# Reordering the copies of an attention stage on one DMA queue, with the copies of the maxima issued by SP

## The reference

```python
cond = silu(c) @ wc.T + bc
sh1, sc1, g1, sh2, sc2, g2 = split(cond, 6)
h = ln(x) * (1 + sc1) + sh1
x = x + g1 * gqa_attn(h, wq, wk, wv, wo)      # softmax(q k / sqrt(32)) v, then wo
h = ln(x) * (1 + sc2) + sh2
x = x + g2 * (gelu(h @ w1.T + b1) @ w2.T + b2)
```

## Time and profile before

| | us |
|---|---|
| median of 3 runs | 1560.06 (1552.71 to 1562.45) |
| profiled execution, own time | 1565.58 |
| its span | 1563.8 |
| PE busy | 1481.9 (95%) |
| DVE / ACT / POOL busy | 800.6 / 625.1 / 576.0 |
| queue of SP: share of 16 DMA engines | 21.7% |
| queue of ACT: share | 0.2% |

### The profile page before, as it was taken

One profiled execution on the slowest core, in us unless ns is written; L12 is line 12 of the kernel. 1 busy time (PEld: TensorE's weight loads), 2 busy tenths in 40 slices (PEclk: granted clock), 3 DMA queues, 4 the chain that ended last, 5 costly groups with the idle time before them and its releaser, 6 DMA issues. The chain is left out here.

```text
span 1563.8 us, 19142 instructions
## 1 busy us (share of the span) xinstructions
PE 1481.9 (95%) x7013; PEld 1045.6 (67%) x7013; DVE 800.6 (51%) x1356; ACT 625.1 (40%) x1116; POOL 576.0 (37%) x222
## 2 busy tenths in 40 slices
PE   7889999998999999998979999999999999999996
PEld 4545556555656555654448888888788888878885
DVE  5377667776776677676544342332524242242421
ACT  5346656665575666666532322112111121211210
POOL 0027567675776677576710020110202021020202
PEclk9869999999999999999999999999999999999998
DMA  7132314233151313323053311010202001020100
GB/s 259 55 75 59 97 52 117 65 85 101 33 154 36 112 54 98 93 71 87 2 158 112 101 55 34 27 60 0 87 0 69 18 27 60 0 87 0 61 1 27
DMA packets 68309, 105.16 MB, mean 67 GB/s; under 512 B 10464, under 2 KB 19696, under 8 KB 68232
## 3 DMA queue, kind: packets, MB, share of 16 engines
q1 hardware_dynamic: 66192, 103.74, 21.7%
q10 hardware_dynamic: 2048, 0.53, 0.2%
HBM read 55.44 MB, written 16.81 MB: 46 GB/s over the span
## 5 line engine op out<-in xcount | busy, mean ns | idle before, releaser
L899 DVE TENSOR_REDUCE neg_max<-row_bank 128x1 f32<-128x512 f32 x512 | 338.5, 683 | 184.1 <-PE row_bank L1095 181.9
L768 ACT ACTIVATE probs<-key_bank 128x512 f32<-128x512 f32 x512 | 301.5, 597 | 224.5 <-PE key_bank L1108 219.6
L1463 PE MATMUL acc<-w_t,hidden 128*128 128x512 f32 x1536 | 370.6, 390 | 7.7 <-DVE hidden L1380 7.7
L1453 PE MATMUL up<-h,w_t 128*128 128x512 f32 x1536 | 370.9, 391 | 0.0
L1463 PEld LDWEIGHTS acc<-w_t,hidden 128*128 128x128 f32 x1536 | 287.3, 188 | 69.8 <-DVE hidden L1380 10.7
L1453 PEld LDWEIGHTS up<-h,w_t 128*128 128x128 f32 x1536 | 287.5, 188 | 58.7
L651 POOL TENSOR_TENSOR probs_sum<-probs_sum,probs 128x2048 f32<-128x2048 f32 x62 | 284.5, 4589 | 29.2 <-ACT probs L768 22.5
L1324 ACT ACTIVATE gelu_full<-up,bias_cols 128x512 f32<-128x512 f32 x128 | 88.3, 690 | 515.2 <-PE up L1453 515.2
L1378 DVE CAST hidden<-gelu_full 128x512 fp32r<-128x512 f32 x128 | 67.2, 525 | 443.4 <-ACT gelu_full L1324 441.7
L1108 PE MATMUL key_bank<-q_stack,k_stack 98*128 98x512 f32 x512 | 227.0, 446 | 21.4 <-DMA q_stack<-max_row 13.3
L1095 PE MATMUL row_bank<-k_stack,q_stack 96*128 96x512 f32 x512 | 212.0, 426 | 10.8 <-DVE neg_max L899 9.5
(11 more groups left out here) (117 smaller groups left out, 1069.0 us busy)
## 6 DMA issues: line engine op xcount, KB each, us to landing
q_stack<-spare SPq DMA_DIRECT2D x384, 64.0 KB, 2.0
xa<-in_x_dram SPq DMA_DIRECT2D x8, 1024.0 KB, 5.1
resid<-in_x_dram SPq DMA_DIRECT2D x8, 1024.0 KB, 7.9
x_scratch<-resid SPq DMA_DIRECT2D x8, 1024.0 KB, 4.4
xa<-x_scratch SPq DMA_DIRECT2D x8, 1024.0 KB, 5.7
spare<-in_L_cond_w_dram SPq DMA_DIRECT2D x32, 256.0 KB, 3.0
resid<-x_scratch SPq DMA_DIRECT2D x8, 1024.0 KB, 6.8
out_dram<-y SPq DMA_DIRECT2D x8, 1024.0 KB, 4.2
```

The source lines that it names most:

```text
L768: nc.scalar.activation(probs[kt][:, r, :], key_bank[r % 2][:, :], ACT.Exp).then_inc(exp_done, 1)
L899: nc.vector.tensor_reduce(out=neg_max[:, g % 2, i:i + 1], in_=row_bank[(g + i) % 2][:, :], op=ALU.max, axis=AX.X, negate=True).then_inc(ro ...
L1453: last = nc.tensor.matmul(up[j % 2][:, :], w1_t[i][:, kt, j * P:j * P + P], h[k][:, kt, :], start=(kt == 0 and n == 0), stop=(kt == KD - 1 ...
L1463: last = nc.tensor.matmul(acc[tt][:, :], hidden[j % 2][i][:, tt * P:tt * P + P], w2_t[k][:, j, :], start=(j == 0 and n == 0), stop=(j == N ...
```

## The change

On SP the copies of the maxima are added (`stack_max` moves there from ACT), and the order of the others is changed. stack_k(3) and stack_q(2) are issued in group 0, stack_q(3) in group 1, stack_q(0) in group 2, stack_q(1) in group 3. The gate and residual of sequence b - 1 are loaded in group 1 of sequence b, behind stack_q(3), after a wait for the last store; the store of b - 1 comes at the end of group 3, behind the maxima of the next sequence. ACT issues nothing any more.

```diff
                 def load_resid(b):
+                    if b > 0:
+                        sp.wait_ge(x1_stored, b * 16)
                     sp.dma_start(gate_now[:, :], gate_dram[bass.ds(b, 1), 0, :].partition_broadcast(P)
                                  .rearrange("p a d -> p (a d)")).then_inc(gate_loaded, 16)
                     sp.dma_start(resid[:, :, :], seq_dram(x, b)).then_inc(resid_loaded, 16)
...
+                def stack_max(b, g):
+                    sp.wait_ge(row_taken, row_no(b, g, ROWS) + 1)
+                    for part in range(2):
+                        row = as_f32(q_stack[STACK + part:STACK + part + 1, g, :, :])
+                        sp.dma_start(row.rearrange("o r n -> o (r n)"), as_f32(max_row[part][:, :])).then_inc(max_stacked, 16)
...
                     stack_q(u, 1)
+                    stack_max(0, 0)
                     stack_k(2)
-                    stack_k(3)
-                    stack_q(u, 2)
...
                     if has_last:
                         sp.wait_ge(keys_scored, exps_no(b, 0, 0))
-                        stack_k(HKV - 1)
+                    stack_k(3)
+                    stack_q(seq_units(b - 1, b > 1, True) if has_last else before_units(), 2)
+                    stack_max(b, 1)
+                    sp.wait_ge(keys_scored, exps_no(b, 1, 0))
                     stack_q(u, 3)
+                    if has_last:
+                        load_resid(b - 1)
                     if has_next:
                         sp.wait_ge(proj_ready, u.ready("T3"))
...
                         sp.wait_ge(proj_taken["dve"], u.taken("K"))
                         stack_k(0)
-                        stack_q(u, 0)
+                    stack_max(b, 2)
+                    if has_next:
                         sp.wait_ge(keys_scored, exps_no(b, 2, 0))
                         stack_k(1)
-                        stack_q(u, 1)
-                    if has_last:
-                        store_x1(b - 1)
-                        sp.wait_ge(x1_stored, b * 16)
-                    load_resid(b)
+                        stack_q(u, 0)
+                    stack_max(b, 3)
                     if has_next:
                         sp.wait_ge(keys_scored, exps_no(b, 3, 0))
                         stack_k(2)
-                        stack_q(u, 2)
+                        stack_q(u, 1)
+                        stack_max(b + 1, 0)
+                    if has_last:
+                        store_x1(b - 1)
...
+                    load_resid(b)
                     for j in range(RING):
                         load_weights(sp, j)
...
-                def stack_max(b, g):
-                    act.wait_ge(row_taken, row_no(b, g, ROWS) + 1)
-                    for part in range(2):
-                        row = as_f32(q_stack[STACK + part:STACK + part + 1, g, :, :])
-                        act.dma_start(row.rearrange("o r n -> o (r n)"), as_f32(max_row[part][:, :])).then_inc(max_stacked, 16)
...
-                    stack_max(0, 0)
...
-                    if n % GROUP == TURN_BEAT + 1 and after_turn:
-                        stack_max(*after_turn)
```

More of the change, by code:

```diff
@@ L587, in before, with sequence @@
                     stack_q(u, 1)
+                    stack_max(0, 0)
                     stack_k(2)
-                    stack_k(3)
-                    stack_q(u, 2)
-                def sequence(b, has_last, has_next, odd=None, is_second_last=False):
+                def sequence(b, has_last, has_next, is_second_last=False):
                     u = seq_units(b, has_last, has_next)
```

## The result

The changed kernel takes 1574.54 us (median of 4 runs, 1573.04 to 1575.9) where the kernel before took 1557.70 in the runs beside it: a ratio of 1.0083, with a 95% interval of 1.0047 to 1.0119. A second comparison of the two, further down, gave 1.0082 (1.0055 to 1.0109). The forecast was 1578, slower.

The account below looks back on a forecast made before the run. PE (TensorE) was taken to bound the kernel. Terms +22.8 + 15.4 - 13.3 - 8.8 - 1.0 = +15.1 us gave 1580.7 from the profiled 1565.6, 1575.2 from the median; 1578 was taken between, range 1556 to 1593.

Parts of the forecast that it names:

- The gate is late, DVE waits, PE waits: Group 1, sequences 1 to 7: gate lands late, delaying DVE's row maximum; PE waits 3.1 us six times, 4.2 once: +22.8 us.
- The clock: Behind PE's seven new waits in group 1: slower clock each time, 2.2 us each, +15.4 us, bounds 0 and 20.
- Store and residual away from the maxima: First scores of new sequences: all five PE waits for maxima go, 13.3 us, plus 8.8 us of slower clock: 22.1 us gained.
- ACT's issues: SP issues the maxima, so ACT loses two issues a group, 1.17 us together; gain taken as 1.0 us, bounds 0 and 5.8.
- Nothing for residual, x load and the one queue: Group 1: later residual and x load cost nothing; maxima behind them on SP's queue still land in time.
- the rival of late maxima: Group 1: maxima behind 2.25 MB on one queue land late, seven times 3.2 + 2.2 us, 1616 us; chance 5%.
- The rivals of a shorter wait: Group 1: clock stays up or gate lands early, about 1560 us, 25%; gate covered, no new wait, 1537 us, 7%.
- The sum: Whole kernel: all gains and costs together, +15.1 us on the profiled execution, 1565.6 to 1580.7; from the median 1575.2.

Follow-up runs that it names:

- the move that undoes it: Changed kernel with the gate issued ahead of the 12 copies of Q3 in group 1, the residual still behind them: 1537.34 us, ratio 0.9833 to the kernel before.
- the kernels with the gate behind nine copies and alone: Changed kernel with gate behind 9 of 12 Q3 copies: 1543.72 us; with gate behind all 12, SP awaiting its landing before residual and x load: 1561.50 us.
- The kernel with this part alone: Kernel before, ACT still issuing maxima, with group 3's store, gate and residual loads moved behind stack_k(2) and stack_q(2): 1542.46 us, ratio 0.9877.

## Why the prediction was right, and where it was off

**The gate is late, DVE waits, PE waits.** Shown in all its steps, by the timelines above and by the move that undoes it (1574.5 to 1537.3 us). In sequence 3 DVE's wait was 4.65 us (4.5 forecast) and PE's 3.24 (3.1 forecast). That they are so near is in part luck, since two errors offset each other: the 12 issues took 8.0 us instead of 7.5, and the gate landed in 4.6 us instead of 5.1. Over seven PE's waits were 24.5 us against 22.8. The q issues, of which one or two were held up in four of the seven sequences, took 3.1 us more than forecast, the landings (4.5 to 5.2 us, 4.8 in the mean, against 5.1) 2.2 us less; the other 0.8 is not traced.

**The clock.** Seven falls, as forecast, at 1.9 us each in place of 2.2: 13.5 us against 15.4. The experiments add the other side: waits of 0.76 us and of 1.4 to 1.7 us brought none in the kernels with the gate behind nine copies and alone.

**Store and residual away from the maxima.** Right in mechanism and size. The kernel with this part alone is 1542.5 us, and its profiled execution is 23 us shorter in span than that of before (1540.4 for 1563.8, of which 1.4 us are an earlier first score), where 22.1 was forecast.

**ACT's issues.** This term of the sum was mis-sized: 1.0 us taken, 5.4 measured in the first groups of sequences 1 to 7. The bound of 5.8 was too low as well. Sequence 0 and the third group of sequence 7 are each 0.5 us shorter in the changed kernel, and in the profile with ACT issuing again they were 0.3 and 0.5 us longer than in the changed one; that makes 6.3 us or so. The prediction read the wait list of PE for exponentials and judged that few of its entries stood behind an issue. What it should have read is ACT's own timeline in the beats of the issues. In group 0 ACT has no idle time there, so that the issues shift all that follows, and PE's list names only a part of that shift.

**Nothing for residual, x load and the one queue.** Right. The copies of the maxima landed in 1.8 to 2.3 us in the changed kernel, so the rival of late maxima fell; POOL's waits for the residual (65.9 us in 7) cost PE nothing in sequences 1 to 6, and PE's one wait for a sum of POOL's in sequence 7, 1.28 us, is as long where the residual is loaded ahead of Q3.

**The rivals of a shorter wait.** The clock stayed up in no sequence, and no gate copy of the changed kernel came in the 3.0 us that a faster kernel needed. The estimate of 2.6 us that the Trainium skill's fit for a DMA issued by GpSimd gives for 256 KB (DMA: Bandwidth & Descriptors, section Anatomy of one DMA) is below every gate copy measured here, even those with nothing large near them, 3.2 us at the least.

**The sum** was +15.1 us. Medians moved by 16.8 us, the two profiled executions by 7.5, half of what the sum gave for them. They moved by less because ACT's term gave 4.4 us more in the first groups, sequence 0 and the third group of sequence 7 another 1.0, the start 1.5, the clock 1.9 and the last groups 0.7 beyond their waits, against 1.7 us of longer waits. The medians moved by more because the profiled execution of the kernel before, with its five waits for the maxima, was itself 8 us over the median of the runs beside the changed kernel, and that of the changed kernel 1.5 us below its own. So the closeness of 1574.5 to 1578, or to the 1575.2 from the median, is in part luck: a gain on ACT that was taken too small met a median of the kernel before 8 us under its profiled execution. The prediction had allowed for a gap of that kind (it took 5.5 us), and not for the gain on ACT.

That an execution of the kernel before has more or fewer of the seven waits, as SP or ACT issues first by some tenths of a us, would explain the 16 us over which its 21 runs beside the experiments spread (1555.22 to 1571.38); only one of its executions was profiled, so this isn't shown. The kernels with neither these waits nor those for the gate, or with two of the latter, spread over 3 to 5 us in four runs each.

## What to carry to other kernels

Before a load is moved down a queue, find its first reader in the trace, and add up what the queue issues ahead of it: here 12 issues of 0.62 us and more, and the landing, put a 256 KB load 4.0 to 6.2 us behind its reader, and what counted of the 12 copies was the time to issue them, since the load landed as fast behind them as without them. Put small loads that are needed early ahead of bursts and of large transfers; here that one line turns a change that costs 0.8% into one that gains 1.7%. Where an engine has no idle time around a DMA that it issues, read what the issue costs from that engine's own timeline rather than from the wait list of the engine that you care for: here two issues, 1.17 us together, cost 0.8 us in each first group, where ACT was full, and 0.1 in each group 1 of sequences 1 to 6.

## What the runs showed of the hardware

- A copy is slowed by what is issued *behind* it, here on its own queue: a 256 KB gate took 3.2 to 3.9 us in 14 copies with nothing or only small copies behind it, 3.5 to 4.3 with a 1 MB load issued 2.4 us behind it, and 3.5 to 5.9 with one issued 0.4 to 0.6 us behind it, where the median of a kernel's eight was 4.4 to 4.8.
- An own queue did not shield the maxima. Beside the residual on ACT's queue the last copies of a pair took 4.9 to 7.5 us; behind it on SP's, 6.4 to 7.8; with nothing large in flight 1.9 by the median on either, 2.8 at most. This agrees with the Trainium skill (DMA: Bandwidth & Descriptors, section Issuing engines are not separate DMA queues): DMAs of all engines interleave on the same 16 DMA engines, and issuing from several saves only the issuing time. The page calls that time usually small relative to the DMA. Here one issue was 0.5 to 0.6 us for a copy that landed in 1.9, and on an engine that was full the issues cost the kernel 5.4 us in the first groups alone.
- Behind the waits of PE at the places studied (first scores and beat 6 of group 1), in all profiles here, the clock fell to 1.2 GHz for 34 of 35 waits of 1.8 us and more and for 1 of 7 between 0.7 and 1.8 us. The exceptions are a wait of 2.7 us without a fall, in the repeated profile of the changed kernel, and one of 1.5 us with a fall, in sequence 0 of the kernel before with SP's maxima. A fall cost 1.1 to 3.1 us, often nearly as much again as a wait of 2 to 3 us. The length of one wait does not decide alone: in sequence 7 of the kernel before with the large transfers late, the clock was low from 751.6 to 755.0 with no wait of PE over 0.5 us ahead of it in that sequence.
